# Upper two merge levels of a block-triangular inverse: off-diagonal blocks only, with the order of the pieces laid out anew

## The reference

```python
def step(S, inp):
    qt, kt, vt, gt, bt = inp
    S = S * jnp.exp(gt)[..., None, None]
    mem = jnp.einsum('bhk,bhkv->bhv', kt, S)
    delta = (vt - mem) * bt[..., None]
    S = S + jnp.einsum('bhk,bhv->bhkv', kt, delta)
    o = jnp.einsum('bhk,bhkv->bhv', qt * scale, S)
    return (S, o)
```

## Time and profile before

| | |
|---|---|
| median of 3 runs | 2455.03 us (2451.66 to 2455.71) |
| span of the profiled execution, first to last instruction | 2456.4 us |
| PE busy | 2237.5 us, 91% |
| DVE busy | 1965.9 us, 80% |
| ACT busy | 1254.7 us, 51% |
| POOL busy | 1428.8 us, 58% |
| `delta_rule` | from 77 to about 2120 us |

### The profile page before, as it was taken

The page is one execution under the profiler, slowest core; times in us unless marked ns, Lnnn a source line. Parts: engine busy times, 40 slices in busy tenths (PEclk is TensorE's granted clock), DMA queues, the critical chain, the costliest instruction groups (busy, mean ns, idle before and its releaser), DMA issues. The chain is left out here.

```text
span 2456.4 us, 51294 instructions
## 1 busy us (share of the span) xinstructions
PE 2237.5 (91%) x17776; PEld 1772.7 (72%) x17776; DVE 1965.9 (80%) x4147; ACT 1254.7 (51%) x3075; POOL 1428.8 (58%) x2174
## 2 busy tenths in 40 slices
PE   6489999999999999999999999999999998799997
PEld 2367777777777777777777777777777777555664
DVE  5678888888888888888888888888888897235544
ACT  4245555555555555555555555555555555222221
POOL 2557777776666777777776666666677666100000
PEclk9689999999999999999999999999999999799998
DMA  4211111112111211121112111211121110301100
GB/s 131 66 29 36 37 56 35 36 37 56 36 36 36 56 37 37 37 56 37 37 37 56 37 37 37 56 37 37 37 56 36 37 26 9 99 32 35 34 9 9
DMA packets 203842, 102.96 MB, mean 42 GB/s; under 512 B 97010, under 2 KB 185019, under 8 KB 203587
## 3 DMA queue, kind: packets, MB, share of 16 engines
q1 hardware_dynamic: 203266, 99.55, 16.9%
q10 hardware_dynamic: 320, 0.13, 0.0%
HBM read 69.79 MB, written 2.54 MB: 29 GB/s over the span
## 5 line engine op out<-in xcount | busy, mean ns | idle before, releaser
L910 DVE SCALAR_TENSOR_TENSOR dr_y<-dr_ps,cw,dr_y 128x255 f32<-128x255 f32 (+2 forms) x1152 | 479.8, 471 | 9.5 <-ACT dr_y L1032 9.5
L774 PE MATMUL dr_ps<-dr_w,dr_am 128*128 128x96 f32 x3072 | 430.1, 283 | 36.6 <-ACT dr_w L1084 36.6
L774 PEld LDWEIGHTS dr_ps<-dr_w,dr_am 128*128 128x128 f32 x3072 | 380.3, 193 | 77.5 <-ACT dr_w L1084 47.9
L1182 POOL TENSOR_TENSOR dr_fo<-dr_vo,dr_nhalf 128x4 f32<-128x4 f32 x128 | 129.5, 1012 | 287.8 <-DVE dr_vo L981 287.7
L1084 ACT COPY dr_w<-dr_ps 128x384 f32<-128x384 f32 x384 | 187.5, 488 | 206.5 <-PE dr_ps L774 206.4
L1032 ACT ACTIVATE dr_y<-dr_ps,cw 128x256 f32<-128x256 f32 x384 | 160.9, 470 | 202.1 <-PE dr_ps L706 202.0
L922 DVE TENSOR_TENSOR_SCAN dr_dec<-dr_abc,dr_dg 128x512 f32<-128x512 f32 x128 | 209.4, 1636 | 19.6 <-issue 16.8
L1140 POOL TENSOR_TENSOR dr_sq<-dr_sy 128x256 f32<-128x256 f32 x128 | 75.8, 613 | 249.5 <-ACT dr_sy L1046 249.5
L706 PE MATMUL dr_ps<-hT,wqk 128*128 128x256 f32 x768 | 198.3, 395 | 20.8 <-PEq L145 20.8
L735 PE MATMUL dr_ps<-wg,hT 128*128 128x384 f32 x512 | 198.4, 511 | 1.9 <-DVE dr_am L954 1.9
L840 PE MATMUL dr_ps<-wo,dr_oT 128*128 128x256 f32 x768 | 195.4, 391 | 1.2 <-ACT dr_oT L1120 1.0
(11 more groups left out here) (213 smaller groups left out, 5153.4 us busy)
## 6 DMA issues: line engine op xcount, KB each, us to landing
dr_abc<-scr_a SPq DMA_DIRECT2D x64, 512.0 KB, 5.4
dr_qk<-dr_sy SPq DMA_DIRECT2D x384, 48.0 KB, 2.0
dr_bcb<-scr_b SPq DMA_DIRECT2D x128, 64.0 KB, 4.7
dr_c<-dr_b SPq DMA_DIRECT2D x512, 4.0 KB, 1.8
dr_qk<-dr_sy SPq DMA_DIRECT2D x128, 32.0 KB, 1.9
ex_modb<-scr_mod SPq DMA_DIRECT2D x4, 1024.0 KB, 8.1
wv<-in_Wv SPq DMA_DIRECT2D x8, 384.0 KB, 3.5
wo<-in_Wo SPq DMA_DIRECT2D x1, 3072.0 KB, 12.1
```

Of the source, the lines that this page charges most:

```text
L774: last = pe.matmul(ps[:, bank, h * DV:(h + 1) * DV], wt(h), x[:, h * DV:(h + 1) * DV], start=(start and h == 0), stop=(h == QH - 1), skip_ ...
L910: v.scalar_tensor_tensor(y[:, slot, x:T], ps[:, BANK[n], off:off + T - x], cw[:, t, TAPS - 1 - x:TAPS - x], y[:, slot, x:T], ALU.mult, ALU ...
```

## The change

The merges at levels 0 and 1 no longer compute whole matrices. `widen` at its last level writes the merged 32 blocks straight into `tf`, and three of four 32 column blocks of the transposed form into `tn`. Level 0: `merge1` multiplies `b16` with the two blocks 0 and 2 of `tn` (64 columns for each matrix, all eight in one bank); DVE multiplies with a mask of 64 columns into the even blocks of `w16`, whose odd ones are set to zero once at the start; `merge2` makes the off-diagonal blocks in both forms (twice 32 columns), and ACT copies them into `tn` and `tf` with three copies of 32 partitions each. Level 1: `merge1` multiplies with 64 columns of `tn`, ACT (not DVE) copies the lower 64 partitions into `w64`, `merge2` gives 64 columns, and ACT copies 64 partitions into `tf`. The two halves g are gone. The table `PLAN` is replaced as a whole; `expand` moves from the end of one stage to the next turn's start. POOL sets `w16` and `w64` to zero at the start, and everybody waits for them (`set_ok` 7 in place of 5).

The new order of the pieces, by place in the turn (stage in brackets): ks, mean 0 (3), gate 0 (1), w0 1 (3), gate 1 (1), expand, narrow1 0 (2), residual 1,0 (3), narrow2 0 (2), gated 0 (3), widen 0 (2), proj 0 (0), keys_scale, block (1), narrow1 1 (2), taps 0,0 (0), delta 1,0, oT 0 (3), narrow2 1 (2), keys_gain (1), proj 1, taps 0,1 (0), widen 1 (2), residual 1,1 (3), merge1 0 (2), root (1), wo 0, acc 0 (3), silu 0, taps 1,0 (0), values 0 (1), taps 1,1 (0), delta 1,1 (3), taps 2,0 (0), merge2 0 (2), proj 2 (0), values 1 (1), silu 1 (0), merge1 1 (2), out 1, mean 1 (3), taps 2,1 (0), merge2 1 (2), norms (0), round 0 (1), gains (0), w0 0 (2), gated 1 (3), rows (1), keys (0), residual 0,0 (2), decays 0, decayed 0,0, decayed 0,1 (0), base (1), silu 2, scores 0 (0), delta 0,0 (2), oT 1 (3), residual 0,1 (2), decays 1, negate 0 (0), wo 1, acc 1 (3), delta 0,1 (2), decayed 1,0, scores 1 (0), state_out (2), decayed 1,1, negate 1 (0).

```diff
 # PE
+            def merge1(st, l):
+                if l == 0:
+                    pe.wait_ge(s["te_ok"], it * (NARROW + 2) + NARROW + 1)
+                else:
+                    pe.wait_ge(s["tq_ok"], (it + 1) * 3)
+                cols = tn[:, :, 0:3:2, :] if l == 0 else tn[:, :, 0:2, :]
+                for u in range(U):
+                    last = pe.matmul(ps[:, X0, u * 2 * HALF:(u + 1) * 2 * HALF], b16[:, m, u, :], cols[:, u],
+                                     start=True, stop=True)
...
+            def merge2(st, l):
+                pe.wait_ge(s["mask_ok"], it * LEVELS + l + 1)
+                if l == 0:
+                    pe.wait_ge(s["te_ok"], (it + 1) * (NARROW + 2))
+                    for u in range(U):
+                        pe.matmul(ps[:, X1, (U + u) * HALF:(U + u + 1) * HALF], tf[:, m, u, :], w16[:, u, 0, :],
+                                  start=True, stop=True)
+                    for u in range(U):
+                        last = pe.matmul(ps[:, X1, u * HALF:(u + 1) * HALF], w16[:, u].rearrange("p g j -> p (g j)"),
+                                         c32[:, u, :], start=True, stop=True)
+                else:
+                    flat = w64[:].rearrange("p u j -> p (u j)")
+                    for u in range(U):
+                        last = pe.matmul(ps[:, X1, u * 2 * HALF:(u + 1) * 2 * HALF], flat[:, u * 2 * HALF:u * 2 * HALF + P],
+                                         tf[:, m, u, 2 * HALF:P], start=True, stop=True)
...
 # DVE
+            def merge1(st, l):
+                if l:
+                    return
+                v.wait_ge(s["p1"], it * LEVELS + 1)
+                v.tensor_tensor(w16[:, :, 0:3:2, :], ps[:, X0, :].rearrange("p (u g j) -> p u g j", u=U, g=2),
+                                bc(mask[:].rearrange("p (g j) -> p g j", g=2), 1, U), ALU.mult).then_inc(s["mask_ok"], 1)
...
                 if l == NARROW - 1:
-                    spread(tn, c32t).then_inc(s["te_ok"], 1)
+                    spread(tn[:], c32t, 3).then_inc(s["te_ok"], 1)
                 turned(c32, c32t).then_inc(s["c32t_ok"], 1)
                 v.wait_ge(s["c32t_ok"], it * (NARROW + 1) + l + 2)
-                spread(tt, c32).then_inc(s["te_ok"], 1)
+                spread(wide(tf[:, m] if l == NARROW - 1 else tt[:]), c32, 4).then_inc(s["te_ok"], 1)
...
 # ACT
+            def merge1(st, l):
+                if l == 0:
+                    return
+                act.wait_ge(s["p1"], (it + 1) * LEVELS)
+                act.copy(w64[2 * HALF:P, 0:U, :], ps[2 * HALF:P, X0, :].rearrange("p (u n) -> p u n", u=U)
+                         ).then_inc(s["mask_ok"], 1)
+            def merge2(st, l):
+                act.wait_ge(s["p3"], it * LEVELS + l + 1)
+                if l == 0:
+                    act.copy(tn[HALF:2 * HALF, :, 0, :], part(HALF, 1)).then_inc(s["tq_ok"], 1)
+                    for lo in (0, 2 * HALF):
+                        act.copy(tf[lo:lo + HALF, m, :, lo + HALF:lo + 2 * HALF], part(lo, 0)).then_inc(s["tq_ok"], 1)
+                else:
+                    act.copy(tf[0:2 * HALF, m, :, 2 * HALF:P], ps[0:2 * HALF, X1, :].rearrange("p (u n) -> p u n", u=U)
+                             ).then_inc(s["tt_ok"], 1)
...
 # POOL
+            pool.memset(w16[:], 0.0).then_inc(s["set_ok"], 1)
+            pool.memset(w64[:], 0.0).then_inc(s["set_ok"], 1)
+            pool.wait_ge(s["set_ok"], 7)
```

More of the change, by code:

```diff
@@ L49 @@
 LEVELS = 2
-LVL0 = 5
+HALF = 4 * BASE
 DEPTH = 4
@@ L62 @@
 ATANH = [1.0 / (2 * k + 1) for k in range(9)]
[L64 to L72, removed]
[4 rows of a table removed]
[L77 to L81, removed]
@@ L83 @@
-C_ID, C_MASK, C_HEAD = 0, P, P * (1 + LEVELS)
+PLAN = ((2.007, ("proj", 0)), (3.511, ("taps", 0, 0)), (4.781, ("proj", 1)), (4.938, ("taps", 0, 1)),
+        (6.464, ("silu", 0)), (6.567, ("taps", 1, 0)), (6.854, ("taps", 1, 1)), (7.567, ("taps", 2, 0)),
+        (7.787, ("proj", 2)), (7.932, ("silu", 1)), (8.777, ("taps", 2, 1)), (9.144, ("norms",)),
+        (9.267, ("gains",)), (9.507, ("keys",)), (9.585, ("decays", 0)), (10.006, ("decayed", 0, 0)),
+        (11.083, ("decayed", 0, 1)), (11.691, ("silu", 2)), (11.979, ("scores", 0)), (13.957, ("decays", 1)),
+        (14.098, ("negate", 0)), (14.636, ("decayed", 1, 0)), (14.739, ("scores", 1)), (14.766, ("decayed", 1, 1)),
+        (14.878, ("negate", 1)), (15.491, ("gate", 0)), (15.895, ("gate", 1)), (17.83, ("keys_scale",)),
+        (18.291, ("block",)), (19.576, ("keys_gain",)), (20.969, ("root",)), (21.687, ("values", 0)),
+        (22.793, ("values", 1)), (24.261, ("round", 0)), (24.479, ("rows",)), (26.588, ("base",)),
[3 rows of a table added]
+        (39.561, ("residual", 0, 0)), (42.214, ("delta", 0, 0)), (43.672, ("residual", 0, 1)),
+        (44.554, ("delta", 0, 1)), (44.749, ("state_out",)), (45.112, ("ks",)), (45.149, ("mean", 0)),
+        (45.535, ("w0", 1)), (46.003, ("residual", 1, 0)), (46.656, ("gated", 0)), (48.739, ("delta", 1, 0)),
+        (49.131, ("oT", 0)), (50.41, ("residual", 1, 1)), (51.36, ("wo", 0)), (51.419, ("acc", 0)),
+        (52.372, ("delta", 1, 1)), (53.581, ("out", 1)), (53.591, ("mean", 1)), (54.452, ("gated", 1)),
+        (57.442, ("oT", 1)), (59.206, ("wo", 1)), (59.227, ("acc", 1)))
@@ L84 @@
+C_ID, C_MASK, C_HEAD = 0, P, P + 2 * HALF
 C_IOTA = C_HEAD + KTL * 2 * QH
@@ L643, in merge2 @@
                     pe.wait_ge(s["te_ok"], (it + 1) * (NARROW + 2))
[L644 to L654, removed]
@@ L687, in narrow2 @@
                 if l == 0:
-                    wait(pe, s["tt_ok"], it * LEVELS * 2)
+                    wait(pe, s["tt_ok"], it)
                 for u in range(U):
@@ L852, in _, with spread @@
             on = {n: nothing for n in PIECES}
[L854 removed]
+            def merge1(st, l):
                 it, m = st
[L856 to L866 removed]
+                if l:
+                    return
+                v.wait_ge(s["p1"], it * LEVELS + 1)
+                wait(v, s["p3"], (it - 1) * LEVELS + 1)
+                v.tensor_tensor(w16[:, :, 0:3:2, :], ps[:, X0, :].rearrange("p (u g j) -> p u g j", u=U, g=2),
+                                bc(mask[:].rearrange("p (g j) -> p g j", g=2), 1, U), ALU.mult).then_inc(s["mask_ok"], 1)
+            def spread(dst, src, blocks):
+                blk = bc(bd32[:, 0:blocks * HALF].rearrange("p (n i) -> p n i", i=HALF), 1, U)
+                return v.tensor_tensor(dst, bc(src[:], 2, blocks), blk, ALU.mult)
             def turned(dst, src):
@@ L878, in expand @@
                 turned(c32t, c32).then_inc(s["c32t_ok"], 1)
-                wait(v, s["p3"], it * LEVELS * 2)
-                spread(tt, c32).then_inc(s["te_ok"], 1)
+                wait(v, s["n2_ps"], it * NARROW)
+                spread(wide(tt[:]), c32, 4).then_inc(s["te_ok"], 1)
             def narrow1(st, l):
@@ L1121, in turn_out @@
                                    scale=gw[:, t:t + 1]).then_inc(s["oT_ok"], 1)
-            on.update(merge2=merge2, rows=rows_, narrow2=narrow2, proj=proj, silu=silu, gate=gate, keys=keys, negate=negate, round=round_,
+            on.update(merge1=merge1, merge2=merge2, rows=rows_, narrow2=narrow2, proj=proj, silu=silu, gate=gate, keys=keys, negate=negate, round=round_,
                       w0=w0, delta=delta, state_out=state, out=squares, ks=ks, oT=turn_out)
             act.wait_ge(s["c_ld"], 32)
-            act.wait_ge(s["set_ok"], 5)
+            act.wait_ge(s["set_ok"], 7)
             run(act, on)
@@ L1663, in constants @@
     c[:, C_ID:C_ID + P] = np.eye(P)
-    for l in range(LEVELS):
-        size = 1 << (LVL0 + l)
-        same = i[:, None] // (2 * size) == i[None, :] // (2 * size)
-        other = i[:, None] // size != i[None, :] // size
-        c[:, C_MASK + l * P:C_MASK + (l + 1) * P] = (same & other) | (i[:, None] == i[None, :])
+    odd = i[:, None] // HALF == 2 * (np.arange(2 * HALF)[None, :] // HALF) + 1
+    c[:, C_MASK:C_MASK + 2 * HALF] = odd
     for n, h, d, t, row, rows in HEAD_ROWS:
```

56 lines of the change are left out of this document (16 added, 40 removed), and 7 rows, old and new, of the table PLAN.

## The result

The changed kernel takes 2434.89 us (median of 6 runs, 2422.13 to 2443.25), the kernel before 2455.37 us (6 runs, 2451.66 to 2458.43). The ratio is 0.9906, with a 95% interval of [0.9884, 0.9928]: 0.9% faster. The forecast was 2348 (2312 to 2392). The sign is right, the size is not, and the runs scatter more than those of before.

The account below looks back on a forecast made before the run. A loop through PE, POOL and DVE was taken to bound the kernel: 5.86 + 11.67 + 2.45 + 2.05 + 7.26 = 29.29 us a turn for 30.97, over 62 turns 104 us less; forecast 2348 us, range 2312 to 2392.

Parts of the forecast that it names:

- the second loop: Chain state_out, ks, mean 0, expand, narrow1 0, residual 1,0, narrow2 0; close behind the binding one, with new PE waits.
- The loop: Round of PE, POOL and DVE from proj 2 to the next proj 2; 30.97 us before, 29.29 forecast.
- the scale: POOL's scaling ahead of gated; power and scale forecast at 2.45 us, with 1.99 as lower bound.
- Widen 0 in the open: DVE's transpose and spread now stand between gated and the narrow mask; that part gets worse by 1.07 us.
- The tail of the turn before: PE from narrow2 1 to the end of proj 2: 9.43 us before, with five merge groups; 7.26 forecast.
- The short scale: Rival: POOL's scale takes 0.83 us beside residual 1,0, giving a turn of 28.83 and 2319 us; chance 0.24.
- the diagonals: POOL's first piece of the loop, forecast to begin 5.86 us behind proj 2, bounds 5.4 and 5.98.
- the selects: POOL's four selects, which end the stretch forecast at an unchanged 11.67 us, bounds 11.2 to 12.1.
- The columns: Busy time of each engine in a turn: savings forecast at PE 1.15, DVE 2.2, ACT 2.3 us.
- a sign of being wrong: PE's wait before narrow2 1 gone: then the second loop or PE itself would bind.
- only PE's column counts: Rival: PE's waits add up as before, a turn gives back only 1.15 us; 2382 us, chance 0.19.
- gain mostly eaten: Rival: the two loops add instead of overlapping, 1 us a turn; 2410 us (2392 to 2450), chance 0.08.

Follow-up runs that it names:

- e1_fill_keys: Changed kernel plus two 512-column matmuls on PE behind rows, where PE waits for keys, results never read; 2349.94 us, 0.9581 of the kernel before.
- e9_late_res_fill2: Kernel before with residual 0,0 moved behind keys, plus two 512-column matmuls, results never read, ahead of the matmuls of rows; 2521.77 us, 1.0280 of before.

## Why the prediction was wrong

- **The step that failed** is one sentence of the part on the second loop: "The clock should not move: PE stays over 90% busy." PE is 92% busy and the clock moves. The share over a whole turn says nothing about the 3 us in which thin matmuls and a wait follow each other. The prediction put new waits near this place and priced them as time only, so its sum has no term for the clock. What it lacked is 81 us: 2348 + 81 = 2429, and the measured median is 2434.89. Holding the clock (e1_fill_keys) gives 2349.94.
- **The loop was right in its parts:** 29.29 forecast, 29.15 in an undisturbed turn, with each term within 0.16 but the scale. That the sums lie only 0.14 apart is in part luck: the scale took 0.46 less, the other terms together 0.32 more. Widen 0 in the open costs 1.08 (1.07 forecast). The tail of the turn before has seven merge groups in the trace, not five; no term was worked out from that count.
- **The short scale** had 0.24, and the mechanism held: 0.83 beside residual 1,0 (POOL at 308.88, DVE at 308.73), as the rule of the Trainium skill ("SBUF — State Buffer", section "Who interferes with whom") has it. The turn did not get to 28.83 for it, since the diagonals began 0.16 later, the selects took 0.08 and the tail 0.07 more.
- **A wait that was overlooked:** keys on PE waits for DVE's second instruction of gains (0.38), because both use one PSUM bank. The forecast had a wait of up to 0.6 there for the DMAs. It costs nothing in the loop, but it is the last piece of the thin stretch.
- **The columns:** PE is busy 27.88 in an undisturbed turn (27.9 forecast), DVE 25.83 (25.4), ACT 17.26 (16.7). ACT's copies cost what was assumed, whatever their partitions: 0.58 for 64x512 (0.592 for 128x512 before), 0.36 for 32x256 (0.37 for 128x256). Before merge2 1 PE waits 0.29 (0.5 forecast); at narrow2 1 0.35 (about 1). In the disturbed turn this last wait is gone, which the prediction had named as a sign of being wrong.
- **The rivals:** "only PE's column counts" did not occur. The time falls into "gain mostly eaten" (2392 to 2450, 0.08), but not by its mechanism; the loops did not add. No rival had the clock in it. The sign came out as the likeliest of the three (faster, 0.93), by a fifth of the gain that was forecast (20 of 107 us).

The cause is shown from four sides: the rows of the clock in disturbed and undisturbed turns of one execution, the loss taken away by work that nobody reads, the same work without effect elsewhere, and the loss made in the kernel before by one moved piece. What stays open: how the thin matmuls and the wait share the blame, since a filler changes both; why some turns are spared (their sequence 29.14, 30.92, 32.10 repeats for long stretches); how the smaller merges bring dips into the old order; and what is left in e9_late_res_fill2.

## What to carry to other kernels

When the order of work on TensorE changes, list the neighbours of its thin pieces (few columns, or a wait) and not only their lengths. A forecast by durations holds as long as the clock does, so look at the mean granted clock and at the lengths of single turns before believing a time. If turns of equal work differ, look for the fall of the clock first, and then for what it sets off: here an engine that came late met another's multiply. Two useless matmuls in a wait cost nothing there and were worth 85 us here.
